# Gated cross-attention and a routed feed-forward layer on one core: shared weights first, the second norm's stage over three engines, late gathers used earlier

## The reference, cut to what matters

```
x = x + tanh(g_xattn) * attention(layernorm(x), ctx, ctx)     # 32 query heads, 8 key/value heads of 16 columns
y = layernorm(x)                                             # the second norm
gate = y @ Wr + br                                           # 7 routed experts, top 2 by gate + gate_bias
out  = sum over the 2 chosen experts of prob * expert(y)     # up 512x512, silu gate 512x512, down 512x512
out += shared expert(y)
x = x + tanh(g_ffn) * out
```

## Time and profile before

| what | us |
|---|---|
| median of 3 runs | 1298.67 (1296.82 to 1299.84) |
| the profiled execution | 1291.94 |
| its span, first to last instruction | 1290.0 |
| attention | 0 to about 342.6 |
| end of attention, second norm's stage | 342.6 to 412.9 |
| early and routed tiles | 412.9 to 1147.9 |
| late tiles | 1147.9 to 1279.2 |
| last sums and the last write | 1279.2 to 1290.0 |
| PE busy | 1199.0 (93%) |
| DVE busy | 853.2 (66%) |
| ACT busy | 586.1 (45%) |
| POOL busy | 376.1 (29%) |

### The profile page before, as it was taken

The page is one execution under the profiler, slowest core; times in us unless marked ns, Lnnn a source line. Parts: engine busy times, 40 slices in busy tenths (PEclk is TensorE's granted clock), DMA queues, the critical chain, the costliest instruction groups (busy, mean ns, idle before and its releaser), DMA issues.

```text
span 1290.0 us, 40478 instructions
## 1 busy us (share of the span) xinstructions
PE 1199.0 (93%) x15170; PEld 894.9 (69%) x15170; DVE 853.2 (66%) x1471; ACT 586.1 (45%) x1131; POOL 376.1 (29%) x453
## 2 busy tenths in 40 slices
PE   3888889999777999999999999999999999999996
PEld 2444445555367777778888888888888888877774
DVE  5889989999776789545545445444444444448887
ACT  3767779898776422233333333333333333322221
POOL 4457666666710000210111111111111011015553
PEclk9889999999977999999999999999999999999998
DMA  5765556565566231644322453226411142267765
GB/s 189 222 226 179 177 177 213 192 208 191 178 215 227 66 131 66 221 159 144 115 81 81 155 182 136 65 65 213 144 58 57 54 151 88 68 198 233 243 189 162
DMA packets 91602, 197.36 MB, mean 153 GB/s; under 512 B 12177, under 2 KB 12689, under 8 KB 91537
## 3 DMA queue, kind: packets, MB, share of 16 engines
q1 hardware_dynamic: 80816, 161.34, 36.6%
q0 software_dynamic: 10720, 35.14, 9.4%
HBM read 332.72 MB, written 64.49 MB: 308 GB/s over the span
## 4 chain that ended last, share of the span: by engine, by line
PE 72%; DVE 12%; issue 5%; DMA 4%; POOL 4%; ACT 2%; DVEq 1%; SPq 0%; ACTq 0%; POOLq 0%
PE PS L1629 41%; PE PS L1667 20%; DVE negm L981 6%; PE PS L1614 3%; PE PS L1449 2%; PE PS L1483 1%; DMA xnd<-xhl 1%; DMA qB<-negT 1%; PE PS L1469 1%; POOL whl L674 1%; DVE wst L1010 1%; DVE xn L967 1%; PE PS L1565 1%; DMA yg<-ysl,ixf 1%; DVE rec L994 1%
## 5 line engine op out<-in xcount | busy, mean ns | idle before, releaser
L1629 PE MATMUL PS<-xT,wb 128*128 128x128 f16 (+1 forms) x4128 | 279.8, 229 | 4.5 <-issue 2.4
L1629 PE MATMUL PS<-uhl,wb 128*128 128x128 f16 (+1 forms) x4128 | 279.8, 229 | 1.9 <-DVE uhl L1239 1.9
L1629 PEld LDWEIGHTS PS<-xT,wb 128*128 128x128 f16 x4128 | 264.0, 98 | 14.0 <-issue 5.4
L1629 PEld LDWEIGHTS PS<-uhl,wb 128*128 128x128 f16 x4128 | 263.5, 98 | 10.8 <-DVE uhl L1239 1.4
L1667 PE MATMUL PS<-wb,ghl 128*128 128x512 f16 x1200 | 267.2, 379 | 0.0
L1667 PEld LDWEIGHTS PS<-wb,ghl 128*128 128x128 f16 x1200 | 115.9, 98 | 130.1
L900 ACT ACTIVATE sl<-PS,bb 128x128 f32<-128x128 f32 (+1 forms) x344 | 106.9, 388 | 188.2 <-PE PS L1629 186.1
L890 ACT ACTIVATE u<-PS,bb 128x128 f32<-128x128 f32 (+1 forms) x344 | 107.0, 388 | 171.5 <-PE PS L1629 166.9
L724 POOL COPY ixr<-idx 128x2 int32 (+1 forms) x35 | 6.4, 184 | 610.5 <-PE PS L1614 610.5
L981 DVE TENSOR_REDUCE negm<-PS 128x8 f16<-128x1024 f32 x128 | 155.1, 1212 | 22.4 <-PE PS L1449 21.5
L1246 DVE TENSOR_TENSOR g<-sl,u 128x512 f32<-128x512 f32 x102 | 70.5, 691 | 150.3 <-ACT sl L900 150.3
(11 more groups left out here) (157 smaller groups left out, 1391.2 us busy)
## 6 DMA issues: line engine op xcount, KB each, us to landing
wb<-wsc SPq DMA_DIRECT2D x219, 1024.0 KB
wst<-in_wall SPq DMA_DIRECT2D x32, 768.0 KB, 5.9
wsc<-whl SPq DMA_DIRECT2D x32, 768.0 KB, 4.3
ysl<-yb SPq DMA_DIRECT2D x43, 512.0 KB
bd<-in_bdown SPq DMA_DIRECT2D x74, 256.0 KB
X<-in_x SPq DMA_DIRECT2D x8, 1024.0 KB, 6.6
qB<-qT SPq DMA_DIRECT2D x32, 256.0 KB, 2.6
xnd<-xhl SPq DMA_DIRECT2D x32, 256.0 KB, 3.3
```

What stands on the lines that cost most here:

```text
L1629: ins = pe.matmul(bank_of(bank, t, m, kind), wb[:, j, l, k, w, m * P:(m + 1) * P], rhs(x, k)[:, ts], start=(n == 0), stop=(n == len(TERMS) ...
```

## The change

- **Weight blocks in another order.** `block_of` rotates the list by four: the shared expert's blocks are passed through first. Its three 1 MB loads (`shared_weights`) are issued by SP in the last batch of attention, behind waits that are all for work of that phase, and ahead of the store of block 30. `store_x2` no longer has weight loads between its parts. The last block's store stands behind the last `store_x2`.
- **The stage divided anew.** ACT writes the high half and copies the transposes of even batches out of PSUM (`evac_x2` in its list). DVE makes the f32 rows (`norm2`, a `tensor_scalar` with two per-row scalars) and copies the transposes of odd batches. POOL subtracts (`low2`); the third `rstd2` stands on POOL behind the first eight of these. DVE makes the last block's low half behind its last copy, ahead of the router's logits and of the first tile's `evac_x`. ACT's first `evac_x` waits for that low half, and its first `up_out` for the last block's store.
- **Late tiles.** Before, `late` = 0 and 1 had `add_routed(late, 0)` at the end of the tile, and the second half (`add_routed(late, 1)`) behind it or in the next tile; `late` = 2 and above had `add_routed(late, 0)` between `gating` and `split_u` and `add_routed(late, 1)` at the end. Now the tile `late` = 0 has `add_routed(0, 0)` ahead of `split_u` and `add_routed(0, 1)` at its end, tile 1 has both halves of group 1 ahead of `split_u` and `add_routed(2, 0)` at its end, and every later tile has `add_routed(late, 1)` ahead of `split_u` and `add_routed(late + 1, 0)` at its end.

The core of the diff:

```
 def body(half, par, quad):                       # SP, attention
+    if isinstance(half, int) and number(half, par) == NB - 1:
+        shared_weights()
...
-            store_x2(0)
-            store_w(NB // 2 - 1, 1, True)
-            store_x2(1)
...
+            for i in range(3):
+                store_x2(i)
             sp.wait_ge(S["x1_ready"], NB)
...
+            low2(0, (0, 1))                       # POOL
             residual(NB // 2 - 1, 1)
+            low2(0, (2, 3))
+            low2(1, range(4))
             rstd2(3)
+            with g.Fori(2, NB // 4) as i:
+                low2(i, range(4))
...
+            def four(i):                          # ACT
+                for k in range(4):
+                    if k % 2 == 0:
+                        evac_x2(i - 1, k)
+                    norm2(i, k, False)
...
+            def four(i, last, late=False):        # DVE
+                for k in range(4):
+                    if not (last and k > 0):
+                        norm2(4 * i + k + 3, (k + 3) % 4)
+                    if k % 2 == 1:
+                        evac_x2(i, k)
...
-                if isinstance(late, int) and late == 1:      # DVE, tiles
-                    add_routed(0, 1)
-                elif late is not None and not isinstance(late, int) or late in (2, N_TILES - 1 - SH_B0):
+                if isinstance(late, int) and late < 2:
                     add_routed(late, 0)
+                if late is not None and following is not None and not (isinstance(late, int) and late == 0):
+                    add_routed(late, 1)
...
-                    if isinstance(late, int) and late < 2:
-                        add_routed(late, 0)
-                    if not (isinstance(late, int) and late == 0):
-                        add_routed(late, 1)
+                    if isinstance(late, int) and late == 0:
+                        add_routed(0, 1)
+                    else:
+                        add_routed(late + 1, 0)
```

More of the change, by code:

```diff
@@ L455, in _ @@
             store_x2(NB // 4 - 1)
+            store_w(NB // 2 - 1, 1, True)
             for j in range(4):
@@ L462, in _ @@
                 store_y(i, i % 2)
+                if i == 0:
+                    for par in range(2):
+                        sp.wait_ge(w_out[par], 16 * (NB // 2))
                 if i < 3:
@@ L902, in gate_out @@
                     ins.then_inc(S["s_ready"], 1)
+            act.wait_ge(S["x1_ready"], NB)
+            act.wait_ge(S["wlo_ready"], NB)
             evac_x(0, 0)
+            for par in range(2):
+                act.wait_ge(w_out[par], 16 * (NB // 2))
             up_out(0, 0, "early", 0)
@@ L1090, in evac_x2 @@
                 need(v, S["gate_done"], b - 1)
-                v.tensor_copy(xhT[:, k % 2, :, :], Rb16[k % 2]).then_inc(x2T[k % 2], 1)
+                v.tensor_copy(xhT[:, 1, :, :], Rb16[1]).then_inc(x2T[1], 1)
+            v.wait_ge(S["ln2_ready"], 2)
+            norm2(0, 0)
+            norm2(1, 1)
             normalise(NB // 2 - 1, 1, 0)
-            low2(0, 0)
             stats2(NB // 2 - 1, 0)
             normalise(NB // 2 - 1, 1, 1)
-            low2(0, 1)
+            norm2(2, 2)
             stats2(NB // 2 - 1, 1)
             means2(3)
+            def four(i, last, late=False):
+                for k in range(4):
+                    if not (last and k > 0):
+                        if late and k == 1:
+                            v.wait_ge(S["ln2_ready"], 3)
+                        norm2(4 * i + k + 3, (k + 3) % 4)
+                    if k % 2 == 1:
+                        evac_x2(i, k)
+            four(0, False)
+            with v.Fori(1, NB // 4 - 2) as i:
+                four(i, False)
+            four(NB // 4 - 2, False, True)
+            four(NB // 4 - 1, True)
             v.wait_ge(S["whi_ready"], NB)
@@ L1102, in _ @@
             v.tensor_tensor(whl[:, 1, :, 1, :], wst[:, 1, :, :], whl[:, 1, :, 0, :], ALU.subtract).then_inc(S["wlo_ready"], 1)
-            def four(i, last):
-                for k in range(4):
-                    evac_x2(i, k)
-                    if not (last and k > 1):
-                        low2(i + (k + 2) // 4, (k + 2) % 4)
-            four(0, False)
-            with v.Fori(1, NB // 4 - 1) as i:
-                four(i, False)
-            four(NB // 4 - 1, True)
             def over_b(ap):
@@ L1359, in tile @@
                     behind_gating(i)
-                if isinstance(late, int) and late == 1:
-                    add_routed(0, 1)
-                elif late is not None and not isinstance(late, int) or late in (2, N_TILES - 1 - SH_B0):
+                if isinstance(late, int) and late < 2:
                     add_routed(late, 0)
+                if late is not None and following is not None and not (isinstance(late, int) and late == 0):
+                    add_routed(late, 1)
+                if late is not None and following is None:
+                    routed_first(late)
                 if following is not None:
@@ L1368, in tile @@
                     add_shared(early, ys[:, par, :])
-                if following is None:
-                    routed_first(late)
                 down_out(i, par, kind, half)
```

74 lines of the change are left out of this document (44 added, 30 removed).

## The result

The changed kernel takes 1289.21 us, the median of 5 runs (1285.02 to 1293.73); 5 runs of the kernel before beside them gave 1299.61 (1296.82 to 1300.68). The ratio is 0.9938, with a 95% interval of 0.9911 to 0.9966: faster, by 0.6%. The profiled execution's span is 1283.3 us, against 1290.0 before: −6.7, where −4.0 was forecast.

What follows compares the result with a forecast made beforehand. PE is busy 93%; around the second norm no engine is full and ACT waits for batch stores, and late gate layers wait behind gathered sums. Stage −4.6 and late tiles +0.6 make −4.0: 1298.67 to 1294.7 us, range 1288.0 to 1302.6.

Steps and rivals of the forecast that it cites:

- More is won: Rival at the second norm: stores slip through beside the loads, pace 1.25; −9.7, 1289.0; or second late stall absent, −7.3; chance 0.26.
- the second late stall: Gate layer of tile 45 waits for the sum (1, 1): 7.9 us late, 3.3 of it new.
- Faster, by the stage: Around the second norm: up layer begins 5.1 us earlier, less 0.5 for PE's clock, so −4.6.
- Start at 360, one long wait: Stage start: ACT may rewrite buffer 0 at 360; this one wait replaces 12.6 us of waits inside the loop.
- Pace 1.36: Stage: POOL's subtraction with a `norm2` of DVE costs 1.16 + 0.20 = 1.36 us a batch; 24 batches take 32.6.
- `rstd2` costs 4.93: Stage: the third `rstd2` on POOL takes 4.93 us, in which no subtraction is made; before it cost nothing.
- The rival of POOL shut out for DVE's whole operation: Stage, every batch from the eighth: pace 1.69, 7.9 us longer, so +3.9, 1302.6, slower; chance 0.18.
- The low half behind the last copy costs 1.64, and a clock loss of 0.5: Stage end: DVE's low half delays the up layer by 1.64 us; PE's lower clock in first tiles 0.5, from 0 to 2.5.
- Late tiles +0.6: Late tiles: stalls ahead of tiles 44 and 45 put PE 5.9 us late, the end gains 5.3; net +0.6.
- The rival of PE at its lower clock through the stage: Stage: PE at a clock of 0.50 is the bound, 3.6 us, so −0.4, 1298.3, no change; chance 0.14.

Runs made afterwards that it cites:

- e7: Changed kernel with only the first of three 1 MB loads ahead of the batch stores, the other two behind the last batch's store: 1290.81 us, ratio 0.9960.
- e4: Changed kernel with the four small bias DMAs moved from behind the 24th batch's store to behind the last one's: 1283.06 us, ratio 0.9902.
- e9: Changed kernel with the stage's work divided as before, bias DMAs behind the last store and late sums placed where their gathers have landed: 1277.86 us, ratio 0.9873.
- e6: Changed kernel with the last block's low half on DVE four batches ahead of the stage's end: 1286.28 us, ratio 0.9929.
- e5: Changed kernel with a third order of the late sums, each placed where its gathers have landed: 1281.97 us, ratio 0.9904.
- e1: Changed kernel with the late tiles' order of before, the stage still divided anew: 1289.07 us, ratio 0.9932.

## Why the prediction was right, and where its sizes were off

The time came out inside the stated range and the way that was forecast, but not where the forecast put it. 1289.21 lies below the forecast's own range, 1291.5 to 1297.7, and beside the rival *More is won*, 1289.0. That rival's conditions held at most in part: the pace was 1.30 and not 1.25, ACT's go-ahead came at 359.59 and not at 356.9, and the second late stall was there. How the terms came out:

- *Faster, by the stage.* Right. Forecast −4.6 for it, first tiles included; measured −9.53 + 1.49 = −8.0 counted from the last residual. Of the 3.4 more, the start is 2.4, `rstd2` 1.7, the way from the last subtraction to the up layer 0.4, and the clock takes 1.0 back.
- *Start at 360, one long wait.* The row came at 359.59 with 3.22, but that is luck. The attention of this execution was 1.74 longer, and from the last residual it is 3.85 instead of 6.0; POOL's `rstd2`, put at 12.3 after that mark, began 9.94 after it (365.68). This is the largest error of the sum. The mechanism was wrong too: e7 shows that an earlier go-ahead leaves POOL's chain where it was, so the landing of the first stores did not set the start.
- *Pace 1.36.* It was 1.30. What a `norm2` costs POOL was read rightly from the earlier trace rows, 0.18 for 0.20, with `norm2` ending 0.29 after the subtraction, as there 0.28. What was mis-sized is what it is added to: subtractions alone start 1.12 apart, not the 1.16 that one takes. And three of the 24 start with no `norm2` running (in e4 the first two and the last), so that 24 take 30.68 without a pause, as e4 shows. The sum of 24 came out as forecast all the same, 32.7, by luck: the pause of 2.41 that e4 traced to the bias DMAs filled the difference. I had looked at the stores and not at the other DMAs that SP issues between them.
- *`rstd2` costs 4.93.* It was 3.19, 365.68 to 368.87. Most of the difference, 1.29, is its second step, 1.13 against 2.42. In the kernel before it had stood beside DVE's low half of the last block:

```profile
357.04 1.76 DVE L1102 TENSOR_TENSOR whl<-wst,whl 128x1536 f16<-128x1536 f32 x1 [0.26 <-ACT whl L804]
...
357.27 2.42 POOL L628 TENSOR_TENSOR ln<-ln,mhalf 128x4 f32<-128x4 f32 x1
```

It began inside DVE's operation and ended 0.89 behind it, so the 4.93 held a wait that the change takes away. In e9, where DVE's low half stands there again, the step takes 2.43 and `rstd2` 4.93. e6 shows the same DVE operation beside POOL's four subtractions, longer by 1.0. The Trainium skill, page "SBUF — State Buffer", section "Who interferes with whom", says that a DVE operation with two SBUF inputs contends with a GpSimd one that reads SBUF; these places agree.
- *The rival of POOL shut out for DVE's whole operation.* It fell: 1.30 is far from 1.69, and DVE is the one that waits more, 0.97 on the mean of 32 `norm2` against 0.525. The same section of the Trainium skill says that whoever starts first holds the port pair and the other fully blocks. In the rows above the subtraction starts first and `norm2` ends just after it, which agrees; POOL's next subtraction loses 0.18, not the 0.525 of a whole `norm2` that 1.69 had added.
- *The low half behind the last copy costs 1.64, and a clock loss of 0.5.* The delay was 4.16 − 2.71 = 1.45. The clock loss was 1.49 in this execution, 1.4 in that of e5, and 0 in those of e1 and e4, with the same idle of 2.5 ahead of the layer; my 0 to 2.5 held it, and what decides between them is open.
- *Late tiles +0.6.* Measured −0.17. The stalls of 4.25 and 2.13 were put at 4.6 and 3.3, the gain at the end at 5.3 (measured 5.5); e1 shows both sides by themselves.
- *The rival of PE at its lower clock through the stage* fell with the 0.92. In e1's trace the clock was low for 8 us near the stage's end, at 0.58.

The median moved by more than the trace, 10.4 against 6.7. The profiled execution lies 7.7 below the median of 1299.61 before and 4.2 below that of 1289.21 after, and the interval of the ratio is as wide as 7 us. So the account holds for the traces: what the loads, the division, the pauses and the two stalls are worth is shown there; the attention's 1.74 is not explained.

## What to carry to other kernels

When a stage is divided anew, price it by the chain of the engine that becomes full, and look for everything that this chain passes, small steps and a queue's transfers for a later stage included: the errors from one `rstd2` and four bias DMAs, 1.7 and 2.4, each weighed as much here as that of the pace, 24 times 0.06. A duration read from a row can hold a wait for a neighbour that the change removes, so look at what the other engine did at that moment. A result that is consumed earlier must also be asked for earlier; place each use by the time from the request, not by the free slot on the engine.

## What was not expected of the hardware

- POOL and DVE disturb each other by order of start. Where the subtraction starts first, DVE's `norm2` is stretched, from 0.525 to 0.97 on the mean, and POOL's pace goes from 1.12 to 1.30. Where DVE starts first, POOL is stretched: by 1.0 beside one DVE subtraction of 1.75 (e6), and by 0.23 beside a `norm2` that began 0.17 ahead of it (358.72) and took its 0.54 in full.
- Four transfers for a later stage, 4 KB and 256 KB, 0.43 to 0.44 of SP's time each, delayed the batch stores behind them enough for a wait of 2.54; the stage was 2.4 shorter without them.
